# The input projection in scaled fp16 parts: scales from sums of maxima, their inverse in the taps, and twelve staging places

## The reference

```python
u = x @ in_proj_w.T + in_proj_b              # 512 -> 1536 columns
u = jnp.transpose(u, (0, 2, 1))
uc = conv(u, short_w)[..., :L] + short_b     # 3 taps along the rows, each channel by itself
x0, x1, v = jnp.split(uc, 3, axis=1)
v = v * x1
v = fftconv(v, filter, filter_bias)          # filter from a small network with three sines
y = v * x0
x = layernorm(x + y.T @ out_proj_w.T + out_proj_b)
x = layernorm(x + ffn(x))                    # silu(gate) * up, then down; integer weights
```

## Time and profile before

| | |
|---|---|
| median of 3 runs | 994.12 us (993.87 to 994.49) |
| profiled execution | 995.0 us, of which the span that the profile shows is 993.2 us |
| mean granted TensorE clock | 0.994 of full |

### The profile page before, as it was taken

One profiled execution on the slowest core, in us unless ns is written; L12 is line 12 of the kernel. 1 busy time (PEld: TensorE's weight loads), 2 busy tenths in 40 slices (PEclk: granted clock), 3 DMA queues, 4 the chain that ended last, 5 costly groups with the idle time before them and its releaser, 6 DMA issues.

```text
span 993.2 us, 17112 instructions
## 1 busy us (share of the span) xinstructions
PE 961.9 (97%) x6099; PEld 761.5 (77%) x6188; DVE 721.9 (73%) x1345; ACT 426.7 (43%) x929; POOL 571.7 (58%) x628
## 2 busy tenths in 40 slices
PE   6999999999999999999999999999999999999996
PEld 5577777878777777778777887777787777777774
DVE  5498876968777687767868677876877677685454
ACT  3676534433353434434443343443334344333342
POOL 3689773755647476464747646465664746575210
PEclk8999999999999999999999999999999999999998
DMA  7655201121122101221102211111111110001100
GB/s 235 206 170 133 49 1 19 26 64 23 43 43 63 20 5 43 44 64 22 44 5 39 64 22 44 32 47 31 21 43 22 44 22 22 23 3 42 43 22 22
DMA packets 98952, 47.96 MB, mean 48 GB/s; under 512 B 80048, under 2 KB 84784, under 8 KB 98868
## 3 DMA queue, kind: packets, MB, share of 16 engines
q1 hardware_dynamic: 98370, 46.79, 18.1%
q10 hardware_dynamic: 498, 0.08, 0.0%
HBM read 32.17 MB, written 8.39 MB: 41 GB/s over the span
## 4 chain that ended last, share of the span: by engine, by line
PE 87%; issue 4%; DVE 3%; POOL 3%; ACT 1%; DMA 1%; SPq 0%; POOLq 0%; DVEq 0%
PE gate_up L1135 14%; PE gate_up L1136 14%; PE bank L995 11%; PE bank L997 11%; PE bank L996 11%; PE down L1148 8%; PE down L1147 5%; PE bank L1095 5%; PE spectrum L995 1%; PE spectrum L996 1%; PE spectrum L997 1%; PE bank L1070 1%; POOL acc L766 1%; DVE tmp L906 1%; DMA x<-in_win 1%
## 5 line engine op out<-in xcount | busy, mean ns | idle before, releaser
L765 POOL TENSOR_TENSOR acc<-acc,tmp 128x256 f32<-128x256 f32 x160 | 123.3, 771 | 150.3 <-DVE tmp L906 138.6
L729 ACT ACTIVATE hid<-gate_up,gate_scale 128x256 f32<-128x256 f32 x176 | 82.7, 470 | 212.5 <-PE gate_up L1136 212.4
L906 DVE TENSOR_TENSOR tmp<-spectrum,filt 128x512 f32<-128x512 f32 x256 | 172.7, 680 | 0.4 <-PE spectrum L997 0.4
L1135 PE MATMUL gate_up<-x2T_hi,wg_sb 128*128 128x256 f16 x704 | 163.4, 273 | 0.0
L1136 PE MATMUL gate_up<-x2T_lo,wg_sb 128*128 128x256 f16 x704 | 163.3, 273 | 0.0
L1135 PE MATMUL gate_up<-x2T_hi,wu_sb 128*128 128x256 f16 x704 | 163.3, 273 | 0.0
L1136 PE MATMUL gate_up<-x2T_lo,wu_sb 128*128 128x256 f16 x704 | 163.3, 273 | 0.0
L759 POOL TENSOR_TENSOR acc<-acc,tmp 128x512 f32<-128x512 f32 x96 | 127.7, 1331 | 61.3 <-DVE tmp L906 60.8
L995 PE MATMUL bank<-xT_hi,win_hi 128*128 128x512 f32 x360 | 149.5, 415 | 2.8 <-POOL win_lo L747 2.5
L997 PE MATMUL bank<-xT_hi,win_lo 128*128 128x512 f32 x360 | 143.5, 399 | 0.0
L996 PE MATMUL bank<-xT_lo,win_hi 128*128 128x512 f32 x360 | 143.0, 397 | 0.0
(11 more groups left out here) (170 smaller groups left out, 1826.8 us busy)
## 6 DMA issues: line engine op xcount, KB each, us to landing
x<-in_x SPq DMA_DIRECT2D x28, 256.0 KB, 2.8
out<-x SPq DMA_DIRECT2D x28, 256.0 KB, 2.1
xstage<-in_x SPq DMA_DIRECT2D x96, 64.0 KB, 2.6
xstage<-in_x SPq DMA_DIRECT2D x12, 256.0 KB, 4.2
x<-in_win SPq DMA_DIRECT2D x12, 256.0 KB, 6.0
acc<-in_decay SPq DMA_DIRECT2D x4, 256.0 KB
x<-in_wout SPq DMA_DIRECT2D x4, 256.0 KB, 2.8
x2T_hi<-in_wu SPq DMA_DIRECT2D x4, 256.0 KB, 3.8
```

The costliest lines, as they stand in the source:

```text
L765: G.tensor_tensor(acc[:, i, 0, :], acc[:, i, 0, :], t[:, 1, :], ALU.subtract)
L906: TT(dst, spectrum[j % 2][:, :, :], k_part, ALU.mult).then_inc(made_done, 1)
L1135: mm(dst, w[:, kb, rows(q)], x2T_hi[:, kb, ts], start=kb == 0, stop=False)
```

## The change

Weights and rows of the input projection become fp16. Since fp16 has a small range, each of the six groups of `win` and each sequence of x is scaled by a power of two before it is split, and the inverse goes into the taps of the short convolution.

- For a scale, DVE takes the greatest absolute value in each partition (`greatest`, a `tensor_reduce` of 128x512 to 128x1; `xmax` four times per sequence, `wmax` twice per group). TensorE multiplies these maxima by a 128x128 tile of ones (`xs`, `ws`), which puts their sum over all partitions into each partition. DVE sums the few columns, keeps the exponent bits, multiplies by a constant and takes the reciprocal (`xscale`, `wscale`: four small operations that wait for each other). `wtaps` multiplies the taps by the inverses (two small operations per group; one per later sequence).
- ACT's copies get a `scale`. DVE's subtraction becomes a `scalar_tensor_tensor` with the same scale, and the low part of `win` moves from POOL to DVE.
- The staging places are 12 in place of 4, so that a place is loaded again only for pieces 12 to 16.
- The first steps of the list are written anew; group 0 stands ahead of the first split, groups 1 to 5 stand in beats 0 to 4 of the first half. From the second sequence on, `xs` takes a bank of the ring, in beat 6 of the odd half ahead (beat 8 for the second sequence).

```diff
+GROUP_OF_FLOAT = {0: 0, 1: 0, 2: 1, 3: 1, 4: 2, 5: 2, 7: 3, 8: 3, 9: 4, 10: 4, 11: 5, 12: 5}
...
+    if n % 2 == 1 and n + 1 < HALVES and beat == (6 if (n + 1) // 2 in BY_SQUARES else 8):
+        steps += [("xs", (n + 1) // 2)]
...
-            steps += [("xturn", following, beat - 2)]
+            steps += [("xmax", following, beat - 2), ("xturn", following, beat - 2)]
...
+    if n == 1 and beat == 6:
+        steps += [("xmax", 1, tb) for tb in range(TB)]
...
+SCALED_IN_BEAT = {0: (1, 2), 1: (3,), 2: (4,), 4: (5,)}
...
+    return [("wmax", k) for k in GROUP_OF_FLOAT if GROUP_OF_FLOAT[k] == g] + [("ws", g), ("wscale", g), ("wtaps", g)]
...
-    steps = [("xt", 0, 0), ("xt", 0, 1), ("xsplit", 0, 0), ("xsplit", 0, 1), ("stage", 0), ("stage", 1), ("xt", 0, 2),
-             ("xt", 0, 3), ("xsplit", 0, 2), ("xsplit", 0, 3), ("net", 0), ("arg", 0), ("bias", ), ("scales", )]
+    steps = [(kind, 0, tb) for tb in range(TB) for kind in ("xt", "xmax")] + [("xs", 0), ("xscale", 0)]
+    steps += [("wmax", 0), ("wmax", 1), ("ws", 0), ("wscale", 0), ("stage", 0), ("stage", 1)]
+    steps += [("xsplit", 0, tb) for tb in range(TB)] + [("wtaps", 0), ("net", 0), ("arg", 0), ("bias", ), ("scales", )]
...
-        win_hi, win_lo = (sb(f"win_{n}", [P, CB, 3 * D], F32R) for n in ("hi", "lo"))
+        win_hi, win_lo = (sb(f"win_{n}", [P, CB, 3 * D], F16) for n in ("hi", "lo"))
...
-        xT_hi, xT_lo = (sb(f"xT_{n}", [P, CB, L], F32R) for n in ("hi", "lo"))
+        xT_hi, xT_lo = (sb(f"xT_{n}", [P, CB, L], F16) for n in ("hi", "lo"))
...
-                if k >= 4:
-                    sp.wait_ge(stage_used, k - 3)
+                if k >= STAGES:
+                    sp.wait_ge(w_lo_done, k - STAGES + 1)
...
+                        act.wait_ge(w_scaled, g + 1)
+                        A(floats[k][1], float_slot(k), ACT.Copy, scale=w_scale[:, g:g + 1]).then_inc(stage_hi, 1)
...
+                    if k not in GROUP_OF_FLOAT:
+                        pool.wait_ge(stage_hi, k + 1)
+                        G.tensor_tensor(lo, float_slot(k), f32(hi), ALU.subtract).then_inc(stage_used, 1)
...
+                    greatest(x_stat[:, s % 2, tb:tb + 1], xstage[:, tb, :]).then_inc(x_max, 1)
...
+                        Vv.tensor_reduce(least, bank_of(k)[:, :TB + 1], axis=mybir.AxisListType.X, op=ALU.add)\
+                            .then_inc(bank_read[bank_index[k]], 1)
+                        dve.wait_ge(*read_of(k))
+                    TS(least.bitcast(I32), least.bitcast(I32), EXPONENT, None, ALU.bitwise_and).then_inc(x_step, 1)
+                    dve.wait_ge(x_step, 2 * s + 1)
+                    TS(least, least, INTO_RANGE, None, ALU.mult).then_inc(x_step, 1)
+                    dve.wait_ge(x_step, 2 * s + 2)
+                    Vv.reciprocal(scale, least).then_inc(x_scaled, 1)
+                    if s:
+                        TS(taps_x[:, s % 2, :, :], taps_w[:, :, :], least, None, ALU.mult).then_inc(taps_set, 1)
...
+                    STT(out=floats[k][2], in0=float_slot(k), scalar=w_scale[:, g:g + 1], in1=floats[k][1],
+                        op0=ALU.mult, op1=ALU.subtract).then_inc(w_lo_done, 1)
...
-                        pe.wait_ge(stage_used, (0, 7)[n] + 2 * t + 2)
+                        pe.wait_ge(w_lo_done, 2 * (3 * n + t) + 2)
...
+                    pe.wait_ge(w_max, 2 * g + 2)
+                    mm(first_sums[:, 8 * g + 8:8 * g + 11], ones[:, :], w_stat[:, g, :], start=True, stop=True)\
+                        .then_inc(sums_done, 1)
```

More of the change, by code:

```diff
@@ L195, in setup_steps @@
     if n == 0:
+        for g in SCALED_IN_BEAT.get(beat, ()):
+            steps += group_steps(g)
         steps += {1: [("sin", 0), ("net", 1), ("arg", 1)], 2: [("sin", 1), ("arg", 2)], 3: [("net", 2), ("sin", 2)],
@@ L313, in build @@
         steps = program()
-        use = count(steps, "xt", "ip", "tv", "iv", "op", "x2t")
+        use = count([s for s in steps if s != ("xs", 0)], "xt", "ip", "tv", "iv", "op", "x2t", "xs")
         convs = count(steps, "conv")
@@ L334, in build @@
         net = sb("net", [P, 4], F32)
+        more_stages = sb("more_stages", [P, STAGES - TB, D], F32)
+        ones = sb("ones", [P, P], F32)
+        x_stat, w_stat = sb("x_stat", [P, 2, TB + 1], F32), sb("w_stat", [P, GROUPS, 3], F32)
+        x_inv, x_scale = (sb(f"x_{n}", [P, 2], F32) for n in ("inv", "scale"))
+        w_inv, w_scale = (sb(f"w_{n}", [P, GROUPS], F32) for n in ("inv", "scale"))
+        taps_w, taps_x = sb("taps_w", [P, 12, TAPS], F32), sb("taps_x", [P, 2, 12, TAPS], F32)
         minus_half = sb("minus_half", [P, 2], F32)
@@ L363, in build @@
         w3_in, inv_in, zeros_set, w_in = (sem(n) for n in ("w3_in", "inv_in", "zeros_set", "w_in"))
-        staged = [sem(f"staged{n}") for n in range(4)]
+        staged = [sem(f"staged{n}") for n in range(STAGES)]
+        ones_set, x_max, w_max = sem("ones_set"), sem("x_max"), sem("w_max")
+        sums_done, sums_read, x_step, w_step = sem("sums_done"), sem("sums_read"), sem("x_step"), sem("w_step")
+        x_scaled, w_scaled, taps_set, w_lo_done = sem("x_scaled"), sem("w_scaled"), sem("taps_set"), sem("w_lo_done")
         code_in = [sem(f"code_in{n}") for n in range(CODE_SLOTS)]
@@ L651, in _ @@
                     s, tb = at
+                    act.wait_ge(x_scaled, s + 1)
+                    scale = x_scale[:, s % 2:s % 2 + 1]
                     if s in BY_SQUARES:
@@ L654, in _ @@
                         act.wait_ge(bank_ready, use["ip", 2 * s - 1, 1, X0] + 1)
-                        A(xT_hi[:, tb, :], turned_block(tb), ACT.Copy).then_inc(x_hi_done, 1)
+                        A(xT_hi[:, tb, :], turned_block(tb), ACT.Copy, scale=scale).then_inc(x_hi_done, 1)
                     else:
@@ L659, in _ @@
                         src = bank_of(k).rearrange("p (c t) -> p c t", c=CB)
-                        A(xT_hi[:, :, rows(tb)], src, ACT.Copy).then_inc(x_hi_done, 1)
+                        A(xT_hi[:, :, rows(tb)], src, ACT.Copy, scale=scale).then_inc(x_hi_done, 1)
                 elif kind == "conv":
@@ L675, in _ @@
                         act.wait_ge(bias_step, 6)
+                    act.wait_ge(taps_set, 3 * n + t + 1 if n < 2 else GROUPS + n // 2)
                     dst = (cv[:, c, :], cx1[:, :], cx0[:, 2 * (n % 2) + c, :])[t]
                     for a, b in ((0, 1), (1, 2), (2, L)):
-                        last = A(dst[:, a:b], bank_of(k)[:, a:b], ACT.Identity, scale=taps[:, q, 2:3],
+                        last = A(dst[:, a:b], bank_of(k)[:, a:b], ACT.Identity, scale=taps_x[:, n // 2 % 2, q, 2:3],
                                  bias=conv_bias[:, min(a, 2), q:q + 1])
@@ L864, in _ @@
                     dve.wait_ge(x_hi_done, TB * s + tb + 1)
+                    scale = x_scale[:, s % 2:s % 2 + 1]
                     if s in BY_SQUARES:
-                        TT(xT_lo[:, tb, :], turned_block(tb), f32(xT_hi[:, tb, :]), ALU.subtract).then_inc(x_lo_done, 1)
+                        STT(out=xT_lo[:, tb, :], in0=turned_block(tb), scalar=scale, in1=xT_hi[:, tb, :],
+                            op0=ALU.mult, op1=ALU.subtract).then_inc(x_lo_done, 1)
                         continue
@@ L869, in _ @@
                     src = bank_of(k).rearrange("p (c t) -> p c t", c=CB)
-                    TT(xT_lo[:, :, rows(tb)], src, f32(xT_hi[:, :, rows(tb)]), ALU.subtract).then_inc(bank_read[bank_index[k]], 1)
+                    STT(out=xT_lo[:, :, rows(tb)], in0=src, scalar=scale, in1=xT_hi[:, :, rows(tb)],
+                        op0=ALU.mult, op1=ALU.subtract).then_inc(bank_read[bank_index[k]], 1)
                 elif kind == "conv":
@@ L1062, in _ @@
                     last.then_inc(bank_ready, 1)
+                elif kind == "xs":
+                    s, = at
+                    dst, done = (first_sums, sums_done) if s == 0 else (free_bank(use["xs", s]), bank_ready)
+                    pe.wait_ge(x_max, TB * (s + 1))
+                    mm(dst[:, :TB + 1], ones[:, :], x_stat[:, s % 2, :], start=True, stop=True).then_inc(done, 1)
+                elif kind == "ws":
+                    g, = at
+                    pe.wait_ge(w_max, 2 * g + 2)
+                    mm(first_sums[:, 8 * g + 8:8 * g + 11], ones[:, :], w_stat[:, g, :], start=True, stop=True)\
+                        .then_inc(sums_done, 1)
                 elif kind == "tv":
```

96 lines of the change are left out of this document (79 added, 17 removed).

## The result

The changed kernel takes 1029.35 us (median, 1028.26 to 1031.3), beside 994.18 for the kernel before on the same chip: ratio 1.0356, 95% interval 1.0338 to 1.0374. Its profiled execution took 1028.64 us with a span of 1026.8, 33.6 more than before. The forecast was 1020; 1029 lies in its range, at the place of rival 4. One later execution (the profiled one of maxima_twice) took 2577.71 us beside 1036.41 to 1037.3 for the other three of that kernel, with the granted clock shown at full, and is left out of every comparison.

What follows compares the result with a forecast made beforehand. TensorE's product length was taken to bound the middle, DVE's and POOL's chain the start. 995.0 + 35.2 at the start - 9.6 in the middle = 1020.6, less 0.9 for the median: 1020 us, range 1005 to 1034.

Steps and rivals of the forecast that it cites:

- rival 4: The middle gains nothing because xmax makes DVE late and the gain goes: 1029 us; 14 in 100.
- Until the first projection: Start: DVE's maxima, scales and subtractions make the first projection begin at 32.7 instead of 12.93, 19.8 us late.
- Until the network's third round: Start, after the first projection: 6.1 us more until the filter network's third round ends, or 3.5 at full clock.
- Until the last taps: Start, up to the last taps before the transposes of v (35.40 before): 5.9 us more.
- The second sequence: Its four maxima, scale and taps go between DVE operations in a busy stretch: 3.4 us more delay.
- The middle: After the start: shorter products gain 17.7 us, bank waits give back 8.1, leaving 9.6 us gained.
- The products gain 17.7: Halves 2 to 15: 84 projections, each 0.21 us shorter by 16-bit products at 0.2157 us, 17.7 us in all.
- The wait for a bank takes 8.1: Six odd halves: the second output projection waits 1.35 us each for taps, because xs shifts the ring's parity.
- The maxima cost nothing: Middle: four xmax per sequence, 0.6 us each, hidden because DVE has 82 us idle in 350.
- Rival 3: No wait for the bank, taps coming earlier relative to TensorE: 6.3 us come back, 1013 us; 16 in 100.
- rivals 1, 2 and 5: Start's delay mostly hidden (4 in 100); short products far below 0.2157 (1 in 100); delay and gain cancel (2 in 100).
- rival 1: Start's delay mostly hidden: only group 0 holds up the first projection, 5.2 us late; 988 us; 4 in 100.

Runs made afterwards that it cites:

- maxima_twice: Changed kernel with every maximum of x of sequences 2 to 7 taken twice, the second into unread columns: 1037.12 us, ratio 1.0414 to the kernel before.
- first_early: Changed kernel with the first input projection moved right behind the first round of the filter's network, ahead of the sums of groups 1 to 3: 1022.62 us.
- fixed_all_pool: Changed kernel with constant scales, the start in the old order, and low parts of weights and of x (sequences 2 to 7) on GpSimd: 980.10 us.
- xs_early: Changed kernel with maxima of x one beat earlier for sequences 2 to 7 and their sum ahead of beat 4's projection: 1022.56 us.
- fixed_w_pool: Changed kernel with constant scales, the start in the old order, and the 12 low parts of the weights on GpSimd instead of DVE: 983.96 us.
- both_early: Changed kernel with both moves: first projection behind the network's first round, and maxima and sum of x earlier: 1016.21 us.
- early_low_pool: Changed kernel with first projection, maxima and sum of x earlier, and low parts of weights and of x from sequence 2 on GpSimd; computed scales: 1008.23 us.
- fixed_scales: Changed kernel with constants for all maxima, sums and computed scales, the start in the old order, low parts still on DVE: 989.62 us.
- one_x_scale: Changed kernel without maxima, sum and scale of x for sequences 1 to 7, which take the first sequence's scale and taps: 1015.90 us.
- four_places: Constant scales and low parts on GpSimd as in fixed_all_pool, with four staging places for the weights in place of twelve: 980.47 us.

## Why the prediction was right, and where it was off

**Until the first projection**: forecast 19.8, measured 18.6. The prices held: maxima 0.59 to 0.64 from start to start, 0.68 for a sum's way to DVE.

**Until the network's third round**: 6.1 more forecast. It ends at 51.91 (51.62 and 0.29), 23.6 after before's 28.29, so 5.1 more. The half clock of the projection ahead of that round, which I chose against 3.5 at full clock, is there (0.50 from 43 to 49); it is the third one, and first_early runs it at full clock.

**Until the last taps**: 5.9 more forecast, 8.7 measured. Missing were the 1.0 that the pair of low parts at 54.60 lost (2.41 where other pairs take 1.41), and DVE's waits of 0.88 and 1.01 for the last filter products, behind another stand of TensorE. **The second sequence**: 3.4 forecast, 3.6 measured from these taps to the first mark (32.4 to 36.0). The start as a whole was right, 36.0 against 35.2 forecast, but by errors that cancel: 1.2 and 1.0 too much, 2.8 and 0.2 too little.

**The middle** is where it failed, at the step "the middle therefore gains 17.7 less 8.1, 9.6 us": between the marks 2.1 against 8.5. By the experiments:

- *The products gain 17.7*: right. Between the marks this is 16.6, and fixed_all_pool gains 18.0 there; the 1.4 beyond I put down to DVE, which has fewer low parts there than in the kernel before (not tried by itself). The 131 ns of the Trainium skill's page, TensorE: Matmul & The Clock Gate, section "Back-to-back issue gap", appear in no run here: the new projections step by 0.216 us.
- *The wait for a bank takes 8.1*: near in sum (7.4, changed to xs_early, of which up to 1.7 is the clock from 148.0), wrong in its parts. The step put 1.35 into each half as a wait of the output projection for taps. That wait is 0.16; the sum's own wait for the residual sum is 0.61, which I had not seen, since the sum takes that bank in the output projection's place; about 4.7 fell in half 3 alone (36.2 late at its first output projection, 40.9 at its second), where the hand-written order leaves nothing between the sum and the next user of the ring, and the clock fell after it.
- *The maxima cost nothing*: off by at most 3.4, which includes the six sums at some 0.3 each and the new wait of 1.59. The rows with 82 us idle in 350 were the wrong measure: doubling the maxima cost 6.0.
- *Not in the sum at all*: 5.2 us (fixed_w_pool to fixed_all_pool) for the low parts of x on DVE. I had priced the scaled subtraction by a row of 0.67 and, as their number stays the same, set nothing down for the middle. They take 0.74, and 1.30 for the first of four where it meets GpSimd, in beats where DVE works without a pause. The size is open: 3.0 from both_early to early_low_pool, 6.1 from fixed_scales to fixed_all_pool, and the 5.2 holds up to 1.7 of clock.

18.0 less 7.4, 3.4 and 5.2 is 2.0, the 2.1 measured. That is no check of the parts: they are steps along one row of kernels and must add up, as long as the 12.9 of one_x_scale and the 12.8 of fixed_w_pool are taken for the same. What the steps show is that each of them, the sum moved, the later scales left out and the low parts moved, brings some of the gain back. So rival 4's time came without rival 4's mechanism: the maxima are the smallest of three parts, and no part alone takes the gain. That the range held 1029 is luck in this respect: its upper end had the lost 9.6 in it, for another reason. Rival 3 fell (there were waits), rivals 1, 2 and 5 too; first_early shows why rival 1's 5.2 for the first projection would not have carried to the end.

## What to carry to other kernels

A product made shorter pays in full only if every engine that feeds it still has room in the same beats; count the replaced operations anew there, not only the added ones, and by the fullest stretch rather than by the idle time of hundreds of microseconds. An extra use of a ring of two banks has two waits, its own for the use two before it and that of the next user for the one just before it; put it where other work lies on both sides, and look at places ordered by hand one by one. Scales that are computed cost most where one engine makes them in order ahead of everything else: here 25 us of start were left after both moves and with the low parts on GpSimd, against 18 that the products gave.

## What the hardware showed that was not expected

DVE and GpSimd held each other up here in operations on two tiles of SBUF. In fixed_scales DVE's low part took 1.30 beside GpSimd's operation at 273.80. In the kernel before the same pair met the other way round, DVE and then GpSimd:

```profile
272.24 0.67 DVE L866 TENSOR_TENSOR xT_lo<-turned,xT_hi 128x512 fp32r<-128x512 f32 x1
```

```profile
271.57 0.73 POOL L765 TENSOR_TENSOR acc<-acc,tmp 128x256 f32<-128x256 f32 x1
272.27 1.23 POOL L766 TENSOR_TENSOR acc<-acc,tmp 128x256 f32<-128x256 f32 x1
```

Here DVE came first and took its usual 0.67, and GpSimd's 0.73 became 1.23. At the start of the changed kernel both paid: the pair of low parts at 54.60 took 2.41, and GpSimd's product beside it:

```profile
54.83 1.63 POOL L795 TENSOR_TENSOR cv<-cv,cx 128x512 f32<-128x512 f32 x1 [24.18 <-DVE cx L991]
```

1.63 where it otherwise takes 1.26 or 1.27. The Trainium skill, SBUF — State Buffer, section "Who interferes with whom", says that a DVE instruction with two SBUF inputs contends with a GpSimd instruction that reads SBUF, and that the order of issue, not the shape of the operation, decides who blocks. These rows agree. It means that a shift of a fraction of a microsecond decides which engine pays, and in the kernel before it was GpSimd, which then still stood 1.29 us before its next operation.

The clock did not fall alike after like stands of TensorE. Near the end fixed_all_pool stands 2.17 us for DVE's `tmp` and then runs at half clock; four_places, the same kernel but for the staging places, stands 2.15 at the same place and keeps its clock:

```profile
876.00:879.40 3.40, 3.26 (x11) 2.29 (x12) 2.67 (x6) 2.04 (x5) 3.24 (x4) 0.50 0.64 217
...
876.00:879.40 3.40, 3.40 (x18) 2.67 (x19) 2.53 (x6) 1.89 (x5) 3.32 (x4) 1.00 0.68 223
```

This is where fixed_all_pool loses 1.5 us after the second mark, and four_places none.
